# A decoder layer on one core: where the turned probabilities of the cross attention land in PSUM, one comparison behind a key copy, and the latent values in later steps

## The chip, the core and the metric

The kernel runs on one core of one Trainium2 chip. The metric is the device time of one execution in microseconds; the median of three runs is given. The float32 work is the same before and after the change.

## The reference, cut to what matters

For each of 8 batch rows of 256 tokens with 256 channels:

```
a    = x + attention(x)          # 16 heads: latent keys, 64 selected keys, window keys, gated sum
x1   = layernorm(a)
x2   = layernorm(x1 + cross(x1, ctx))   # 16 heads of width 16, 256 x 256 probabilities each
out  = layernorm(x2 + experts(x2))      # 8 experts, 1024 wide, mixed by a router

cross: q = x1 Wq + bq, k = ctx Wk + bk, v = ctx Wv + bv
       p = softmax(q k' / 4) per head ; out = concat(p v) Wo + bo
latent values of the self attention: v1 = rms(x w_ckv) w_dv     # 256 x 512 per row
```

## The kernel before

One program holds an attention stage over the 8 batch rows and an expert stage after it. The order of the work on every engine is written out by hand, as generators for TensorE (`pe`), VectorE (`dve`), ScalarE (`act`) and GpSimd (`pool`), which meet in semaphores. A row has three parts: `front(i)` (projections, rotary parts, selection of 64 tokens, turned keys and queries), `heads(i)` (16 heads of self attention) and `cross(i)` (16 heads of cross attention, in steps h = 0 to 19). `interleave` runs one step of the front of row i+1 after each step of the last heads and of the cross part of row i, but for three steps (`BREATHERS`). From h = 16 on, the first heads of row i+1 run too. The last row has no front of another row beside it; the first transposes and router scores of the expert stage run there instead.

PSUM has eight banks: S0 to S3, T0, T1, O and X. A `BankPlan` numbers the uses of each bank; a writer waits until the use before it has been read (`free_S0`), a reader until the bank is full (`full_S0`). One cross head h goes through these steps:

- TensorE writes the scores of two heads at once, of h and h+1 for even h, into S0 and S1 (`scores_x`, line 1380 of the profile, `ps_S<-kx_sb,qx_sb`). It waits for both banks.
- VectorE reads them, takes the maximum (lines 1294 and 1300), ScalarE exponentiates (871), VectorE inverts the sum (1174), GpSimd scales (651).
- TensorE turns the probabilities of head h in step h+3 (`turn_probs_x`, 1715), always into the single bank T0 (in the last row into T0 and T1 in turn, by the plan `late`).
- ScalarE copies them to SBUF (883), or VectorE does for heads 1, 5, 9, 13, 14 and 15 (`VECTOR_TURNS`, 1310). After each four heads TensorE multiplies with the values (`ps_O<-pT_sb,vx`).

Of the front, four things matter. `turn_rows` (1435) turns keys and queries, alternately into X and T1. VectorE copies the keys in T1 out (1012), and in the same steps makes two pairs of comparisons for the selection, `beaten_by(0)` and `beaten_by(1)` (1031, 1033). `latent_values(0)` and `(1)` are products of 32 rows into S3 (1380, `ps_S<-w_qd,latT_sb 32*128`), which ScalarE scales into SBUF (703, `v_sb`). Between them stand three products of one column, the places of the selected tokens (`pos`, `ps_S<-sel,upper`). The products of the selected keys and values (`ps_S<-w_ks,lat`) come later, and last the transposes of the selected keys (`turn_rows(4)`, `ps_X<-ident,rot 64*96`).

Of the kernel before, what the change touches and what calls it, by code (L numbers as in the profile page):

```python
# [16 lines left out]
NB, T, C = 8, 256, 256  # L17
NT = T // P
NC = C // P
NH = 16  # L20
# [139 lines left out]
def block_plan(full, free):  # L160

    plan = BankPlan(full, free)
    for h in range(NH):
        for half in range(2):
            if h >= HEAD_START:
                plan.add(("s", h, half), f"S{2 * (h % 2) + half}")
        for half in range(2):
            plan.add(("pT", h, half), f"T{half}")
    for g in range(4):
        plan.add(("o", g), ("X", "O")[g % 2])  # L170
    plan.add("proj", "S0")
    plan.add("ctxT", "O")
    plan.add("kx", "S0")
    plan.add("vx", "S1")
    plan.add("x1T", "T0")
    plan.add("qx", "S0")
    for h in range(NH):
        plan.add(("sx", h), f"S{h % 2}")
        plan.add(("pxT", h), "T0")
    for g in range(2):  # L180
        plan.add(("ox", g), "O")
    plan.add("projx", "O")


    for n, name in enumerate((
# [5 lines left out]
        plan.add(name, f"S{2 + n % 2}", ahead=True)  # L191
    for n, name in enumerate((
            "xT", ("kwT", 0, 0), ("kwT", 0, 1), ("kwT", 0, 2), "latT", ("kwT", 0, 3),
            *(("kwT", 1, g) for g in range(4)), *(("qT", t, g) for t in range(NT) for g in range(4)),
            ("ksT", 0), ("ksT", 1))):
        plan.add(name, ("X", "T1")[n % 2], ahead=True)
    for h in range(HEAD_START):
        for half in range(2):
            plan.add(("s", h, half), f"S{2 * (h % 2) + half}", ahead=True)
    return plan  # L200
# [68 lines left out]
def attention_stage(nc, outer, block, sh, w):  # L269

    ctx = ExitStack()
    with ctx:
# [8 lines left out]
        plan = block_plan({b: sem(f"full_{b}") for b in BANKS}, {b: sem(f"free_{b}") for b in BANKS})  # L281

        def ps(name):
            return pst[plan.bank(name)]

        LATE_BANKS = ("T0", "T1", "S2", "S3", "X")
        late = BankPlan({b: sem(f"late_full_{b}") for b in LATE_BANKS},
                        {b: sem(f"late_free_{b}") for b in LATE_BANKS})
        for h in range(NH):
            late.add(("pxT", h), f"T{h % 2}")  # L290
        for n, name in enumerate((*(("x2T", j, c) for j in range(EARLY) for c in range(NC)),
                                  *(("route", j) for j in range(EARLY)))):
            late.add(name, ("S2", "S3", "X")[n % 3])

        def px(i, h):

            return (late, ("pxT", h), 0) if i == NB - 1 else (plan, ("pxT", h), i)


        w_first = sb("w_first", [P, NC, PA])  # L300
# [43 lines left out]
        gate = sb("gate_sb", [P, 4])  # L344
# [4 lines left out]
        pos = sb("pos_sb", [P, NT])  # L349
# [3 lines left out]
        rot, qT, kT, v1, vw, vs = sh.rot, sh.qT, sh.kT, sh.v1, sh.vw, sh.vs  # L353
# [337 lines left out]
        def _(act):  # L691
# [6 lines left out]
            def evacuate(i, name, dst, src, scale=None):  # L698
                act.wait_ge(plan.full_sem(name), plan.after(name, i))
                if scale is None:  # L700
                    ins = act.copy(dst, src)  # L701
                else:
                    ins = act.activation(dst, src, ACT.Copy, scale=scale)
                ins.then_inc(plan.free_sem(name), 1)
                return ins

            def front(i):
# [26 lines left out]
                def values_out(name, t, dst, scale):  # L734
                    evacuate(i, (name, t), dst[:, t, :], ps((name, t))[:, :], scale)
# [37 lines left out]
                if i:  # L773
# [5 lines left out]
                absorbed(1)  # L779
                query_turn(0, 0)  # L780
                yield
                values_out("v1", 0, v1, gate[:, 0:1])
                query_turn(0, 2)
                yield

                values_out("v1", 1, v1, gate[:, 0:1])
                query_turn(1, 0)
                yield
                query_turn(1, 2)
# [4 lines left out]
                nope(4)  # L794
                evacuate(i, ("ks", "nv"), vs[:, :], ps(("ks", "nv"))[KEEP:2 * KEEP, :], gate[KEEP:2 * KEEP, 1:2])
                yield
                yield

                evacuate(i, ("ksT", 0), kT[:, 0:8, 0:KEEP],
                         ps(("ksT", 0))[0:QK, :].rearrange("p (h t) -> p h t", h=8))  # L800

# [149 lines left out]
        def _(dve):  # L951
# [21 lines left out]
            def front(i):  # L973
# [35 lines left out]
                def key_turn(t, g):  # L1009
                    f = ("kwT", t, g)  # L1010
                    dve.wait_ge(plan.full_sem(f), plan.after(f, i))
                    dve.tensor_copy(kT[:, 4 * g:4 * g + 4, KEEP + P * t:KEEP + P * t + P],
                                    ps(f)[0:QK, :].rearrange("p (h t) -> p h t", h=4)).then_inc(plan.free_sem(f), 1)
# [16 lines left out]
                def beaten_by(t):  # L1030
                    dve.tensor_scalar(cmp1[:, t, :], srow[:, :], scol[:, t:t + 1], None, ALU.is_gt
                                      ).then_inc(c.step(), 1)
                    dve.scalar_tensor_tensor(cmp2[:, t, :], srow[:, :], scol[:, t:t + 1], tie[:, t, :],
                                             ALU.is_equal, ALU.mult).then_inc(c.step(), 1)
# [66 lines left out]
                dve.tensor_copy(latT[0:QL, 0, :], ps("latT")[0:QL, 0:T])  # L1101
                dve.tensor_copy(latT[:, 1, :], ps("latT")[:, T:2 * T]).then_inc(plan.free_sem("latT"), 1)
                own_scores()
                beaten_by(0)
                yield

                key_turn(0, 3)
                beaten_by(1)
                yield

# [264 lines left out]
        def _(pe):  # L1375
# [9 lines left out]
            for h in range(NH):  # L1385
                last = mm(pst["S0"][0:QL, HD * h:HD * h + HD], stage[:, QL * h:QL * h + QL],
                          stage[:, NH * QL + HD * h:NH * QL + HD * h + HD])
# [25 lines left out]
            def front(i):  # L1413
# [44 lines left out]
                def latent_values(t):  # L1458
                    product(i, ("v1", t), P, HW, [latT[QK:P, 1, P * t:P * t + P]], [w_dv[QK:P, :]])
# [9 lines left out]
                for t in range(NT):  # L1469
                    for c in range(NC):  # L1470
                        last = mm(ps("first")[:, T * t:T * t + PA], xT[:, c, P * t:P * t + P], w_first[:, c, :],
                                  c == 0, c == NC - 1)
# [59 lines left out]
                yield  # L1532

                turn_rows(2, (2, 3))
                latent_values(0)
                pe.wait_ge(sel_sb.sem, sel_sb.at(i, 1))
                pe.wait_ge(plan.free_sem("pos"), plan.before("pos", i))
                mm(ps("pos")[:, 0:1], upper[:, :], sel[:, 0:1])
# [1 line left out]
                mm(ps("pos")[:, 1:2], upper[:, :], sel[:, 1:2], False, True).then_inc(plan.full_sem("pos"), 1)  # L1540
                yield

                latent_values(1)
                turn_rows(3, (0, 1))
                yield

# [16 lines left out]

                selected(("ks", "nv"), [w_ks[:, c, 0, :] for c in range(NC)], [w_vs[:, c, :] for c in range(NC)])
                yield
                yield

                turn_rows(4, (0, 1))

            def scores(i, h):  # L1570
# [245 lines left out]
    def end(turns, f, i):  # L1816

        return turns.free_sem(f), turns.after(f, i)

    last = NB - 1  # L1820
    banks = {"S0": end(plan, ("sx", NH - 2), last), "S1": end(plan, ("sx", NH - 1), last),
             "S2": end(late, ("route", 0), 0), "S3": end(late, ("route", 1), 0), "X": end(late, ("route", 2), 0),
             "T0": end(late, ("pxT", NH - 2), 0), "T1": end(late, ("pxT", NH - 1), 0),
             "O": end(plan, "projx", last)}
# [515 lines left out]
```

## Time and profile before

| | us |
|---|---|
| median of 3 runs (lowest, highest) | 1892.19 (1890.14, 1893.77) |
| the profiled execution, its time | 1895.1 |
| its span, first to last instruction | 1893.4 |
| attention stage, until the first expert product | 1148.2 |
| expert stage | 745.2 |

The profile has for each engine the busy time, for each wait its releaser, and for each instruction a start and a duration. "PEclk" is the TensorE clock granted, as a share of 2.4 GHz: 1.00 or 0.50 at any moment. The time of the profiled execution is 1.7 us more than its span and 2.9 us above the median.

### The profile page before, as it was taken

What the parts mean: (1) busy time and instruction counts of PE and PEld (TensorE: products, weight loads), DVE (VectorE), ACT (ScalarE), POOL (GpSimd) and SP (SyncE); (2) the same over time, 40 slices, a digit from 0 to 9 for tenths busy, and PEclk for the clock granted to TensorE, in tenths of its full rate; (3) what the DMA queues carried; (4) which work ended last, traced back from release to release, by engine and by line L of the source; (5) the groups of instructions that cost most, each with busy time, mean ns of one, the idle gap of its engine ahead of it and who ended that gap; (6) DMA issues with size and microseconds to landing.
All of it is one profiled execution on the core that took longest, in us unless ns stands there. A gap on an engine that the chain in (4) does not pass through costs nothing. (4 is left out here: it accounts for less than half of the span.)

```text
span 1893.4 us, 33996 instructions
## 1 busy us (share of the span) xinstructions
PE 1776.1 (94%) x11560; PEld 1372.9 (73%) x11560; DVE 1167.2 (62%) x3980; ACT 888.8 (47%) x2839; POOL 1040.3 (55%) x1447
## 2 busy tenths in 40 slices
PE   7899999999999998999999979999999999999998
PEld 4565665665765765755756747889999999898997
DVE  4568768868867867867777766444543354436335
ACT  1475765856845846936936863222222222213221
POOL 2354554654744745735735638456565566547643
PEclk9799899999998999999999988899999999999999
DMA  5000000000000000000000001010101011010001
GB/s 167 6 1 7 7 2 7 7 8 7 2 7 7 2 7 7 2 7 7 2 7 1 13 35 45 1 45 1 45 1 45 1 45 45 1 42 4 1 1 45
DMA packets 24492, 32.86 MB, mean 17 GB/s; under 512 B 5048, under 2 KB 20928, under 8 KB 24320
## 3 DMA queue, kind: packets, MB, share of 16 engines
q1 hardware_dynamic: 24320, 30.69, 4.9%
q8 instruction: 93, 1.52, 0.3%
q14 instruction: 79, 0.65, 0.1%
HBM read 28.58 MB, written 2.10 MB: 16 GB/s over the span
## 5 line engine op out<-in xcount | busy, mean ns | idle before, releaser
L1942 POOL TENSOR_TENSOR h_lo<-h_sb,h_hi 128x512 fp32r<-128x512 f32 x256 | 360.3, 1433 | 157.5 <-DVE h_hi L2112 157.5
L1990 ACT ACTIVATE h_sb<-ps_H,b_sb 128x512 f32<-128x512 f32 x256 | 176.1, 688 | 523.2 <-PE ps_H L2149 510.1
L616 POOL TENSOR_TENSOR pr<-pr,rden 128x128 f32<-128x128 f32 (+2 forms) x768 | 307.8, 435 | 117.5 <-DVE rden L1174 117.5
L818 ACT ACTIVATE pr<-sm,nmx 128x128 f32<-128x128 f32 (+2 forms) x768 | 311.6, 411 | 33.0 <-DVE nmx L1193 32.9
L2112 DVE CAST h_hi<-h_sb 128x512 fp32r<-128x512 f32 x256 | 221.4, 879 | 157.5 <-ACT h_sb L1990 156.8
L2149 PE MATMUL ps_Y<-w_hi,h_lo 128*128 128x256 f32 x1024 | 288.0, 281 | 0.0
L2149 PE MATMUL ps_Y<-w_hi,h_hi 128*128 128x256 f32 x1024 | 288.0, 281 | 0.0
L2149 PE MATMUL ps_Y<-w_lo,h_hi 128*128 128x256 f32 x1024 | 287.7, 281 | 0.0
L651 POOL TENSOR_TENSOR pr<-pr,rden 128x256 f32<-128x256 f32 x256 | 156.7, 634 | 218.1 <-DVE rden L1174 218.1
L1185 DVE CUSTOM_DVE_ANT_0 sm<-ps_S,cmask 128x128 f32<-128x128 f32 (+2 forms) x768 | 191.4, 307 | 35.8 <-PE ps_S L1380 26.5
L2094 DVE SCALAR_TENSOR_TENSOR x<-ps_Y,route_t,x 128x256 f32<-128x256 f32 x128 | 61.3, 482 | 235.6 <-PE ps_Y L2149 235.6
L2149 PE MATMUL ps_H<-x_hi,w_hi 128*128 128x512 f32 x512 | 203.4, 397 | 0.1
L2149 PE MATMUL ps_H<-x_lo,w_hi 128*128 128x512 f32 x512 | 202.6, 396 | 0.0
L2149 PE MATMUL ps_H<-x_hi,w_lo 128*128 128x512 f32 x512 | 202.5, 396 | 0.0
L2149 PEld LDWEIGHTS ps_Y<-w_hi,h_hi 128*128 128x128 f32 x1024 | 194.5, 190 | 1.3
L2149 PEld LDWEIGHTS ps_Y<-w_lo,h_hi 128*128 128x128 f32 x1024 | 194.5, 190 | 1.2
L2149 PEld LDWEIGHTS ps_Y<-w_hi,h_lo 128*128 128x128 f32 x1024 | 194.5, 190 | 0.0
L871 ACT ACTIVATE pr<-sm,nmx 128x256 f32<-128x256 f32 x256 | 128.1, 502 | 88.9 <-DVE nmx L1300 88.9
L1603 PE MATMUL ps_T<-ident,pr 128*128 128x128 f32 (+1 forms) x1024 | 135.3, 275 | 21.1 <-DVE pT_sb L1205 6.7
L1603 PEld LDWEIGHTS ps_T<-ident,pr 128*128 128x128 f32 (+1 forms) x1024 | 109.8, 133 | 52.7 <-issue 36.6
L818 ACT ACTIVATION_READ_ACCUMULATOR pr<-sm,nmx 128x1 f32 x768 | 147.0, 191 | 0.0
L1380 PE MATMUL ps_S<-latT_sb,qT_sb 128*128 128x128 f32 (+1 forms) x512 | 129.6, 336 | 5.2 <-ACT kT_sb L701 4.2
(246 smaller groups left out, 3281.3 us busy)
## 6 DMA issues: line engine op xcount, KB each, us to landing
w_raw<-in_W SPq DMA_DIRECT2D x16, 1024.0 KB, 6.2
xin<-in_x SPq DMA_DIRECT2D x8, 256.0 KB, 2.9
cin<-in_ctx SPq DMA_DIRECT2D x8, 256.0 KB, 2.6
out<-x SPq DMA_DIRECT2D x4, 512.0 KB, 3.0
w_kw<-in_wink SPq DMA_DIRECT2D x2, 768.0 KB, 6.6
w_ks<-in_selk SPq DMA_DIRECT2D x2, 768.0 KB, 10.0
w_qd<-in_dq SPq DMA_DIRECT2D x1, 576.0 KB, 4.8
w_vw<-in_winv SPq DMA_DIRECT2D x1, 512.0 KB, 8.0
```

The costliest lines, as they stand in the source:

```text
L616: last = pool.tensor_tensor(p_, p_, rden[:, h % 2, n:n + 1].to_broadcast([P, width]), ALU.mult)
L651: last = pool.tensor_tensor(p_, p_, rden[:, h % 2, q:q + 1].to_broadcast([P, T]), ALU.mult)
L818: last = act.activation(pr[:, h % PR_SLOTS, a:a + width], sm[:, h % 2, a:a + width], ACT.Exp, bias=nmx[:, h % 2, n:n + 1], scale=ATT_SCALE ...
L871: last = act.activation(prx[:, h % PR_SLOTS, T * q:T * q + T], smx[:, h % 2, T * q:T * q + T], ACT.Exp, bias=nmx[:, h % 2, q:q + 1], scale ...
L1185: ins = dve.tensor_tensor_reduce(out=sm[:, h % 2, a:a + width], in0=ps(f)[:, off:off + width], in1=cmask[:, m:m + width], scale=1.0, scala ...
L1380: return pe.matmul(out, lhsT, rhs, start=start, stop=stop)
L1603: last = pe.transpose(ps(f)[0:width, dst:dst + P], p[:, a:a + width], ident[:, :])
L1942: pool.tensor_tensor(h_lo[:, s % 2, ht, :], h_sb[:, ht % 4, :], h_hi[:, s % 2, ht, :].bitcast(F32), ALU.subtract).then_inc(lo_sb.sem, 1)
L1990: ins = act.activation(h_sb[:, ht % 4, :], pst[plan.bank(f)][:, :], ACT.Relu, bias=b1[:, 2 * i + s // NCH, ht:ht + 1])
L2094: dve.scalar_tensor_tensor(x2[:, tile, :], pst[plan.bank(f)][:, 0:C], rt[:, 2 * i + s // NCH, tile:tile + 1], x2[:, tile, :], ALU.mult, AL ...
L2112: dve.tensor_copy(h_hi[:, s % 2, ht, :], h_sb[:, ht % 4, :]).then_inc(hi_sb.sem, 1)
L2149: return pe.matmul(out_, lhsT, rhs, start=start, stop=stop)
```

## The change

Three edits. (1) In the bank plan the turned probabilities of the even cross heads 0 to 12 go to S0 in place of T0, between the score pairs that use S0; the odd heads and head 14 stay on T0. In the last row the heads that stay now alternate over T0 and T1, and the even ones go to S0 as well. (2) VectorE's `beaten_by(0)` moves from the step of the latent copy to the next step, behind the key copy `key_turn(0, 3)`. (3) The two latent values and their copies move from the steps around `pos` to the two steps after the selected keys and values, and in the plan of S2 and S3 they stand last.

```diff
@@ block_plan
-    for h in range(NH):
-        plan.add(("sx", h), f"S{h % 2}")
-        plan.add(("pxT", h), "T0")
+    for k in range(NH + 3):
+        if k < NH and k % 2 == 0:
+            plan.add(("sx", k), "S0")
+            plan.add(("sx", k + 1), "S1")
+        if k >= 3:
+            h = k - 3
+            plan.add(("pxT", h), "S0" if h % 2 == 0 and k < NH else "T0")
...
-            ("v1", 0), "pos", ("v1", 1), "xsel", ("ks", "ab"), ("ks", "nv"))):
+            "pos", "xsel", ("ks", "ab"), ("ks", "nv"), ("v1", 0), ("v1", 1))):
@@ attention_stage
-        for h in range(NH):
-            late.add(("pxT", h), f"T{h % 2}")
+        ONE_BANK = [h for h in range(NH) if plan.bank(("pxT", h)) == "T0"]
+        for n, h in enumerate(ONE_BANK):
+            late.add(("pxT", h), f"T{n % 2}")
...
-            return (late, ("pxT", h), 0) if i == NB - 1 else (plan, ("pxT", h), i)
+            return (late, ("pxT", h), 0) if i == NB - 1 and h in ONE_BANK else (plan, ("pxT", h), i)
@@ ScalarE, front
-                values_out("v1", 0, v1, gate[:, 0:1])
                 query_turn(0, 2)
                 yield
-                values_out("v1", 1, v1, gate[:, 0:1])
                 query_turn(1, 0)
...
                 evacuate(i, ("ks", "nv"), vs[:, :], ps(("ks", "nv"))[KEEP:2 * KEEP, :], gate[KEEP:2 * KEEP, 1:2])
                 yield
-                yield
+                values_out("v1", 0, v1, gate[:, 0:1])
+                yield
+                values_out("v1", 1, v1, gate[:, 0:1])
@@ VectorE, front
                 own_scores()
-                beaten_by(0)
                 yield
                 key_turn(0, 3)
+                beaten_by(0)
                 beaten_by(1)
@@ TensorE, front
                 turn_rows(2, (2, 3))
-                latent_values(0)
                 pe.wait_ge(sel_sb.sem, sel_sb.at(i, 1))
...
-                latent_values(1)
                 turn_rows(3, (0, 1))
...
                 selected(("ks", "nv"), ...)
                 yield
-                yield
+                latent_values(0)
+                yield
+                latent_values(1)
                 turn_rows(4, (0, 1))
```

How the instructions stand now. First TensorE in cross steps 8 and 9, from the query transposes into T1 to those into X: `w_qd` is a latent value, `sel` the places, `ident,pr` turned probabilities of head 6. Before:

```order
L1435 MATMUL ps_T1<-ident,rot_57 128x128 [waits free_T1]
L1435 MATMUL ps_T1<-ident,rot_57 128x128 x3
L1380 MATMUL ps_S3<-w_qd_49,latT_sb 128x512 [waits free_S3]
L1380 MATMUL ps_S2<-sel,upper 128x1 [waits free_S2,sel_sb]
L1380 MATMUL ps_S2<-sel,ones 128x1
L1380 MATMUL ps_S2<-sel,upper 128x1
L1715 MATMUL ps_T0<-ident,pr 128x128 [waits free_T0,prob_sb]
L1715 MATMUL ps_T0<-ident,pr 128x128 x3
L1380 MATMUL ps_S3<-w_qd_49,latT_sb 128x512 [waits free_S3]
L1435 MATMUL ps_X<-ident,rot_57 128x128 [waits rope_out,free_X,free_S2,free_S3]
```

The same place in the changed kernel:

```order
L1441 MATMUL ps_T1<-ident,rot_57 128x128 [waits free_T1]
L1441 MATMUL ps_T1<-ident,rot_57 128x128 x3
L1386 MATMUL ps_S3<-sel,upper 128x1 [waits free_S3,sel_sb]
L1386 MATMUL ps_S3<-sel,ones 128x1
L1386 MATMUL ps_S3<-sel,upper 128x1
L1722 MATMUL ps_S0<-ident,pr 128x128 [waits free_S0,prob_sb]
L1722 MATMUL ps_S0<-ident,pr 128x128 x3
L1441 MATMUL ps_X<-ident,rot_57 128x128 [waits rope_out,free_X,free_S2,free_S3]
```

Both latent values are gone from here, and head 6 goes to S0. Second, TensorE from cross step 14 (heads 11 and 12 turned) to the transposes of the selected keys. Before:

```order
L1715 MATMUL ps_T0<-ident,pr 128x128 [waits free_T0,prob_sb]
L1715 MATMUL ps_T0<-ident,pr 128x128 x3
L1715 MATMUL ps_T0<-ident,pr 128x128 [waits free_T0,prob_sb]
L1715 MATMUL ps_T0<-ident,pr 128x128 x3
L1380 MATMUL ps_O<-pT_sb,vx 32x256 [waits free_T0,free_O]
L1380 MATMUL ps_O<-pT_sb,vx 32x256 x7
L1435 MATMUL ps_X<-ident,rot_57 96x64 [waits free_X,sel_nope,rope_out]
```

The same place in the changed kernel:

```order
L1722 MATMUL ps_T0<-ident,pr 128x128 [waits free_T0,prob_sb]
L1722 MATMUL ps_T0<-ident,pr 128x128 x3
L1386 MATMUL ps_S3<-w_qd_49,latT_sb 128x512 [waits free_S3]
L1722 MATMUL ps_S0<-ident,pr 128x128 [waits free_S0,prob_sb]
L1722 MATMUL ps_S0<-ident,pr 128x128 x3
L1386 MATMUL ps_O<-pT_sb,vx 32x256 [waits free_T0,free_S0,free_O]
L1386 MATMUL ps_O<-pT_sb,vx 32x256 x7
L1386 MATMUL ps_S2<-w_qd_49,latT_sb 128x512 [waits free_S2]
L1441 MATMUL ps_X<-ident,rot_57 96x64 [waits free_X,sel_nope,rope_out]
```

The first latent value now stands between the turned heads 11 and 12, the second behind the value products of heads 8 to 11. Third, VectorE around the scores of cross heads 2 and 3, in the changed kernel alone:

```order
L1033 TENSOR_REDUCE scol<-cmp1 128x2 [waits dve_front_chain]
L1300 ISA sm,mx<-ps_S0,sm 128x256 [waits full_S0,dve_front_chain,exp_done]
...
L1306 TENSOR_SCALAR nmx<-mx 128x2 [waits free_S1]
L1018 COPY kT_sb_59<-ps_T1 96x4x128 [waits full_T1]
L1037 TENSOR_SCALAR cmp1<-srow,scol 128x256
L1039 SCALAR_TENSOR_TENSOR cmp2<-srow,scol,tie 128x256
L1037 TENSOR_SCALAR cmp1<-srow,scol 128x256
L1039 SCALAR_TENSOR_TENSOR cmp2<-srow,scol,tie 128x256
```

Before, one pair of comparisons stood between the first two of these rows, ahead of the scores and the key copy; now both pairs stand behind the copy.

## Rows read from the trace of the kernel before

**Rows 1.** The page: busy time, share and instructions of each engine.

```profile
PE 1776.1 (94%) x11560; PEld 1372.9 (73%) x11560; DVE 1167.2 (62%) x3980; ACT 888.8 (47%) x2839; POOL 1040.3 (55%) x1447
```

**Rows 2.** Waits of TensorE, whole span: total us, times, longest us.

```profile
PE ps_T L1715 <- DVE pT_sb L1310: 14.3, 21, 0.8
...
PE ps_T L1435 <- DVE kT_sb L1012: 9.3, 8, 1.2
...
PE ps_T L1715 <- ACT pT_sb L883: 5.8, 7, 0.8
```

**Rows 3.** Batch rows as windows: start, end, length, TensorE busy, granted clock, DMA.

```profile
157.00:295.40 138.40, 128.25 (x851) 0.96 0.02 5
295.40:429.10 133.70, 123.59 (x854) 1.00 0.02 6
...
563.10:701.80 138.70, 128.31 (x851) 0.96 0.02 5
...
835.40:972.30 136.90, 126.82 (x853) 0.98 0.02 6
...
1100.10:1148.20 48.10, 38.69 (x231) 0.76 0.00 1
```

**Rows 4.** Windows at three of the four falls of the clock, columns as above.

```profile
189.40:199.70 10.30, 10.30 (x49) 0.50 0.11 28
...
868.70:875.50 6.80, 6.80 (x33) 0.50 0.02 6
...
1005.20:1012.00 6.80, 6.80 (x33) 0.50 0.00 1
```

**Rows 5.** Timeline, TensorE, second batch row: start, us, what, idle before, releaser.

```profile
304.89 0.61 PE L1435 MATMUL ps_T<-ident,rot 128*96 128x128 f32 x4 [1.24 <-DVE kT_sb L1012]
...
312.31 0.63 PE L1715 MATMUL ps_T<-ident,pr 128*128 128x128 f32 x4 [0.84 <-DVE pT_sb L1310]
...
315.08 1.98 PE L1380 MATMUL ps_S<-w_qd,latT_sb 96*128 96x512 f32 x4 [0.48 <-ACT rot L717]
```

**Rows 6.** Timeline, TensorE, later in the same batch row.

```profile
324.19 1.12 PE L1380 MATMUL ps_S<-w_qd,latT_sb 32*128 32x512 f32 x2
325.24 0.38 PE L1380 MATMUL ps_S<-sel,upper 128*128 128x1 f32 x2
...
326.46 0.63 PE L1715 MATMUL ps_T<-ident,pr 128*128 128x128 f32 x4 [0.39 <-DVE pT_sb L1310]
...
338.29 0.63 PE L1715 MATMUL ps_T<-ident,pr 128*128 128x128 f32 x4 [0.80 <-DVE pT_sb L1310]
...
343.26 0.63 PE L1715 MATMUL ps_T<-ident,pr 128*128 128x128 f32 x4 [0.82 <-ACT pT_sb L883]
...
347.20 0.46 PE L1380 MATMUL ps_S<-latT_sb,qT_sb 128*128 128x128 f32 x2 [0.60 <-ACT kT_sb L701]
```

**Rows 7.** Timeline, VectorE and ScalarE, same batch row.

```profile
301.15 0.35 DVE L1031 TENSOR_SCALAR cmp<-srow,scol 128x256 f32<-128x256 f32 x1
...
301.82 0.41 DVE L1294 CUSTOM_DVE_ANT_0 sm<-ps_S,sm 128x256 f32<-128x256 f32 x1
...
319.88 0.67 DVE L995 TENSOR_TENSOR rt<-ps_S,cs 128x512 f32<-128x512 f32 x1
...
325.40 0.67 ACT L703 ACTIVATE v_sb<-ps_S,gate_sb 128x512 f32<-128x512 f32 x1
...
346.38 0.56 ACT L701 COPY kT_sb<-ps_X 96x512 f32<-96x512 f32 x1
```

**Rows 8.** Timeline, last batch row.

```profile
1112.94 0.56 ACT L883 COPY pT_sb<-ps_T 128x512 f32<-128x512 f32 x1
1112.96 1.13 PE L1380 MATMUL ps_S<-kx_sb,qx_sb 32*128 32x256 f32 x8 [1.82 <-DVE mx L1294]
...
1131.06 1.13 PE L1380 MATMUL ps_S<-kx_sb,qx_sb 32*128 32x256 f32 x8 [1.18 <-DVE mx L1294]
...
1134.31 1.04 ACT L945 CAST w_hi<-w_raw 128x1024 fp32r<-128x1024 f32 x1
```

More of the change, by code:

```diff
@@ L1820, in attention_stage @@
     last = NB - 1
-    banks = {"S0": end(plan, ("sx", NH - 2), last), "S1": end(plan, ("sx", NH - 1), last),
+    banks = {"S0": end(plan, ("pxT", NH - 4), last), "S1": end(plan, ("sx", NH - 1), last),
              "S2": end(late, ("route", 0), 0), "S3": end(late, ("route", 1), 0), "X": end(late, ("route", 2), 0),
```

## The prediction

> **What bounds the kernel now.** I read the page first. TensorE is busy for 94% of the span [rows 1], so a gain must come from its waits or from its clock. The expert stage (745.2 us) is untouched. In the attention stage the list of waits shows where TensorE stands still [rows 2]: 14.3 + 5.8 us before it turns cross probabilities, because the one bank T0 still holds the head before, and 9.3 us before it turns a key block, because VectorE has not copied the last one out of T1. The counts (21, 7 and 8 or 7 per kind) say that the same waits come back in each of the seven batch rows with a following front. The windows by batch row say the same in another way [rows 3]: a row takes 133.7 us at clock 1.00, and 138.4, 138.7 and 136.9 us where the clock was at half for a part. These parts are whole stretches at 0.50, that is 1.2 GHz: 10.3 us, or 6.8 us twice [rows 4]; a fourth, in the row from 563.1, is of the length of the first. So there are two things to win: waits of a few tenths, and falls of the clock that cost 4.7, 5.0 and 3.2 us each, and 3.2 more for the last one, which is as long as the third: 16.1 us in all.
>
> **The change, part by part.** I follow one batch row, the second, by the timeline of TensorE.
>
> *The comparison.* VectorE now starts the scores of heads 2 and 3, and behind them the key copy, at 301.15 and not at 301.82 [rows 7]: 0.67 us earlier. The wait of 1.24 us before the key transposes [rows 5] shrinks to 0.57. The comparisons themselves come back behind the copy, before VectorE's next work, so VectorE has no less to do. Gain here 0.67.
>
> *What holds it at 0.6 for a while.* From there VectorE has hardly a gap until its last rotary product of this stretch, at 319.88 for 0.67 us [rows 7], and TensorE's next query product needs the bank that this one frees. VectorE starts this chain some 0.6 us earlier, so that point comes 0.6 earlier, whatever waits TensorE lost before. Two of them do go (0.84 and 0.48 [rows 5]). The first only moves: head 2 may now be turned at once, but the score pair behind it needs S0, which ScalarE has yet to copy (about 0.7 us for the end of the transposes and the copy). The second goes because that copy is earlier. Neither counts in the sum.
>
> *The latent values leave the steps around the places.* Each costs 1.05 us from its start to the next (324.19 to 325.24 [rows 6]); two are 2.1. The wait of 0.39 for T0 behind them goes too. But they covered something: the query transposes that follow need X, copied by ScalarE, and T1, copied by VectorE, whose own clock hands are only 0.6 early. I count 0.9 us of new waits at these two, from when those copies end. At the score pair of heads 10 and 11 TensorE is early by 0.6 + 2.1 + 0.4 - 0.9 = 2.2 us.
>
> *Late steps.* The wait of 0.80 before head 10 goes: its bank S0 was read long before. The one of 0.82 before head 12 (1.0 from start to start) is filled by the first latent value, 1.05. The second adds 1.05: 2.2 + 0.8 + 1.0 - 2.1 = 1.9 us early. The last wait, 0.60 before the next row's first scores [rows 6], has ScalarE's key copy in it (346.38, 0.56). ScalarE now does two latent copies of 0.67 [rows 7] in these steps, the second directly ahead of that copy; I find its end 1.9 to 2.0 early, so the wait stays near 0.6. The last steps' S3 and S2 are free in time: the rotary products of the selected keys end about 0.8 us before the first latent value wants S3. Behind this point every engine is early by the same amount, and the rest of the row keeps its waits. **Per row 1.95 us, in seven rows 13.7.** Bounds of the row: 0.6, if VectorE's chain holds throughout, and 3.3, the sum of the four waits for T0 and the part of T1's that I take (0.84 + 0.39 + 0.80 + 0.82, and 0.67), less small ones.
>
> *The last row.* Nothing of a front runs beside it, and 48.1 us are mostly latency. There T0 and T1 in turn never held the heads back; now every even head shares S0 with the scores. The pair of heads 6 and 7 starts at 1112.96, when VectorE has read the banks; in the changed kernel it also waits for ScalarE's copy of head 2, which ran 1112.94 to 1113.50 [rows 8]: 0.6 late. The next pairs wait likewise, and ScalarE's weight casts of 1.04 us stand ahead of two of those copies [rows 8], so the pair at 1131.06 may be 4 us late. ScalarE's exponentials had slack behind it, and I carry about half through to the end: **3 us lost**, between 0.5 (the first pair alone) and 5.
>
> *The clock.* In all four rows that show a fall, and in these alone the row is long, it comes at 32 to 33 us behind the first cross scores: right behind latent value, one-column places, wait, turned head, latent value [rows 6]. The three other rows ran the same without a fall. The change takes both latent values and one wait out of that stretch, which then holds transposes with three short waits. It also makes a new thin stretch: the second latent value, the short transposes of the selected keys, one turned head and the wait of 0.6. It is shorter than the old one, so I expect a fall in one or two of seven rows and not in four. **I take 9 of the 16.1 us back**; bounds 16 and minus 12 (falls of 4 us in all seven rows: 28 against 16.1).
>
> The Trainium skill ("TensorE: Matmul & The Clock Gate", "A second HAM failure mode: psum-queue depth-cycling") says that short idles between groups, from cycling through PSUM banks, make the clock swing between its two levels. By that rule fewer waits for a bank leave fewer falls, but the new waits at X and T1 in the same stretch could keep them all; the sum would then be 1881.5. The trace agrees in part: the falls come behind a stretch with such a wait, yet longer waits elsewhere in the row brought none.
>
> The start-up front of the first row has no cross part beside it; the moved products lie there under GpSimd's rotary sums. I count nothing.
>
> Sum: -13.7 - 9 + 3 = -19.7 us. Against the profiled execution, 1895.1 us, that is 1875.4. The median of before is 2.9 lower, as other executions have other falls of the clock, and the change is judged by the median: **1872.5 us**.
>
> **The rivals.**
> - *Waits go, the clock stays as it was* (four falls, by new waits in the old stretch or by the new thin one). For it: the stretch keeps the places and gets two waits. 1892.2 - 13.7 + 3 = 1881.5. Chance 0.17.
> - *VectorE holds all back.* Only the comparison counts: 7 x 0.6 = 4.2, less 3 in the last row, and no fall saved: 1891. For it: VectorE's chain sets four of the meeting points. Against it: after 320.6 us VectorE waits for TensorE's scores again. Chance 0.06.
> - *Slower: S0 makes the score pairs late.* Each pair from head 4 on must wait until ScalarE has copied the even head before. It bites where the copy ends after TensorE reaches the pair; for heads 6 and 7 it does (a pause of 0.7 in place of 0.84), for heads 8, 10 and 14 there is over 1 us of other work between, for 12 and 13 only 0.2 us of margin. If ScalarE runs later than I find by more than 1 us, six pairs in seven rows wait some 0.5: 21 us. With the last row's 3 and the 13.7 gained: about 1902. Chance 0.05.
> - *Slower or equal by the clock alone*: a fall in every row: -13.7 + 12 + 3, 1893.5. Chance 0.06.
> - *No place for the gain*: a later wait takes up most of it. Each engine is shifted alike at the row's end, so little speaks for it: 1889. Chance 0.02.
>
> **How the numbers follow.** My case has the other 0.64, with a range of its own of 1864 to 1881: waits between 10 and 17, clock between 4 and 16, last row 0.5 to 5. With the first rival inside, 1863 to 1884 leaves two in ten out, above all on the slow side. A measurement of this kernel tells 0.2% (3.8 us) from no change. Faster by more: my case and the first rival and a little of the others, 0.82; same 0.11 (the clock rival, VectorE and the last one among them); slower 0.07.
>
> **What the profile of the changed kernel would show.** The wait of the key transposes on VectorE near 0.6; waits of `ps_T` for its copies gone from heads 6, 10 and 12; a wait of some 0.7 before the scores of heads 6 and 7; batch rows of about 131.8 us at clock 1.00; windows at 0.50 in fewer rows, and then near 46 to 50 us behind the first cross scores; a last row of about 51 us. I would be wrong if rows at clock 1.00 took over 133, or if the score pairs showed waits on ScalarE's copies in each step.

## The result and the profile after

Measured beside each other, the kernel before took 1892.01 us (median; 1890.14 to 1893.77) and the changed one 1863.19 us (1860.3 to 1866.08): a ratio of 0.9848, with an interval of 0.983 to 0.9866. That is 9.3 us below my number and only 0.2 us inside the range of 1863 to 1884; the 1864 that I had as the least of my own case is missed. The profiled execution of the changed kernel took 1863.8 us, span 1862.1; so 31.3 us of span are to be explained, not 28.8.

The page's busy times of the changed kernel, the line that answers to [rows 1]:

```profile
PE 1756.3 (94%) x11560; PEld 1359.8 (73%) x11560; DVE 1168.3 (63%) x3980; ACT 888.6 (48%) x2839; POOL 1042.2 (56%) x1447
```

TensorE runs as many instructions as before and is busy 19.8 us less. No product was taken away, so these 19.8 us are the clock's: the same work at 2.4 GHz and not at 1.2. The rest of the 31.3, some 11.5, are waits. VectorE, ScalarE and GpSimd are busy as before.

The list of TensorE's waits in the changed kernel (total us, times, longest us), which answers to [rows 2]:

```profile
PE ps_S L1386 <- issue: 7.3, 10, 1.1
...
PE ps_X L1441 <- ACT qT_sb L706: 6.9, 8, 1.3
...
PE ps_T L1441 <- DVE kT_sb L1018: 5.8, 8, 0.8
...
PE ps_S L1386 <- DVE kT_sb L1169: 3.5, 8, 0.9
PE ps_S L1722 <- DVE mx L1300: 3.4, 9, 0.5
PE ps_S L1386 <- DVE pr L1001: 2.9, 8, 0.4
PE ps_S L1386 <- ACT pT_sb L889: 2.8, 2, 2.1
...
PE ps_T L1722 <- DVE pT_sb L1316: 0.4, 1, 0.4
```

The 14.3 us in 21 waits for VectorE's copy of T0 are one wait of 0.4, and the 5.8 us for ScalarE's are gone. The key transposes wait 5.8 and not 9.3. In their place stand new, smaller ones: for X (6.9; 1.3 before), before score pairs (7.3 with the releaser "issue", which means that the profile shows none; 0.72 of it in each row with a front is the pair of heads 6 and 7, below), and for S0 until its scores are read (3.4). The wait before the next row's scores isn't new: it was 4.2 for ScalarE's copy and 0.9 for VectorE's, and is 3.5 for VectorE's.

The same batch rows as windows, with the columns of [rows 3], and under them two falls of the clock, as in [rows 4]:

```profile
281.20:412.90 131.70, 123.19 (x851) 1.00 0.02 6
676.70:809.70 133.00, 124.67 (x851) 0.99 0.02 5
809.70:942.70 133.00, 124.68 (x851) 0.99 0.02 6
1065.40:1117.00 51.60, 40.19 (x230) 0.77 0.00 1
726.70:730.10 3.40, 3.40 (x12) 0.50 0.00 0
859.80:863.20 3.40, 3.40 (x12) 0.51 0.00 0
```

A row at full clock takes 131.7 us, 2.0 less than the 133.7 of [rows 3]; with the marks to the hundredth, the second row went from 133.62 to 131.72, 1.90 less. Two of seven rows have a fall, 50 us behind their first cross scores and 3.4 us long, where four had one at 32 us, 6.8 or 10.2 long. Unlike in [rows 3], the last row is longer: 51.6 for 48.1.

By marks in the trace the 31.3 us divide so:

| stretch (marks: first cross scores of a row, first expert product) | before | after | difference |
|---|---|---|---|
| start to the first row's cross scores | 157.0 | 149.5 | -7.5 |
| seven rows with a following front | 943.1 | 915.9 | -27.2 |
| last row | 48.1 | 51.6 | +3.5 |
| expert stage | 745.2 | 745.1 | -0.1 |

The 27.2 divide again by a second profile of the changed kernel, told below, in which no row fell: there the seven rows take 913.5. Before, they take 943.1 less 16.1 of falls, 927.0. So the waits gave 13.5 and the clock 13.7.

TensorE's timeline in the second batch row, which answers to [rows 5, 6] (this batch row starts at 281.2 and not at 295.4):

```profile
290.15 0.61 PE L1441 MATMUL ps_T<-ident,rot 128*96 128x128 f32 x4 [0.77 <-DVE kT_sb L1018]
...
297.89 1.13 PE L1386 MATMUL ps_S<-kx_sb,qx_sb 32*128 32x256 f32 x8 [0.72 <-issue]
...
309.37 0.28 PE L1386 MATMUL ps_S<-sel,upper 128*128 128x1 f32 x2
...
309.73 0.36 PE L1386 MATMUL ps_S<-sel,upper 128*128 128x1 f32 x2
309.95 0.63 PE L1722 MATMUL ps_S<-ident,pr 128*128 128x128 f32 x4
311.39 0.63 PE L1441 MATMUL ps_X<-ident,rot 128*128 128x128 f32 x4 [0.81 <-ACT qT_sb L706]
312.25 0.65 PE L1441 MATMUL ps_T<-ident,rot 128*128 128x128 f32 x4 [0.23 <-DVE qT_sb L1024]
...
331.02 0.46 PE L1386 MATMUL ps_S<-latT_sb,qT_sb 128*128 128x128 f32 x2 [0.39 <-DVE kT_sb L1169]
```

The turned head behind the places now goes to S0 (`ps_S<-ident,pr`) and waits for nothing. Of the waits that the prediction named, that of the key transposes is 0.77 (it said 0.57), that before the scores of heads 6 and 7 0.72 (0.7), and those at X and T1 together 1.04 (0.9). For the 0.72 the profile names no releaser; ScalarE's copy out of S0 ran from 297.20 to 297.79, and the pair starts at 297.89. The wait before the next row's scores is 0.39, and it comes from VectorE's half of the selected keys, no longer from ScalarE's.

### The profile page after: what moved, and what is told of

It reads as the page before. It is cut to its first block and busy times, and to the rows that moved or that the text cites. A ratio compares the mean times of both kernels' runs of the same rounds, so it can differ in the third digit from the quotient of the medians.

```text
span 1862.1 us, 34004 instructions
## 1 busy us (share of the span) xinstructions
PE 1756.3 (94%) x11560; PEld 1359.8 (73%) x11560; DVE 1168.3 (63%) x3980; ACT 888.6 (48%) x2839; POOL 1042.2 (56%) x1447
## 5 line engine op out<-in xcount | busy, mean ns | idle before, releaser
L1191 DVE CUSTOM_DVE_ANT_0 sm<-ps_S,cmask 128x128 f32<-128x128 f32 (+2 forms) x768 | 191.6, 308 | 35.1 <-PE ps_S L1386 19.7
L1386 PE MATMUL ps_S<-kT_sb,qT_sb 96*128 96x320 f32 (+1 forms) x512 | 134.6, 386 | 0.0
```

The source lines that it names most:

```text
L1191: ins = dve.tensor_tensor_reduce(out=sm[:, h % 2, a:a + width], in0=ps(f)[:, off:off + width], in1=cmask[:, m:m + width], scale=1.0, scala ...
L1386: return pe.matmul(out, lhsT, rhs, start=start, stop=stop)
```

## The experiments

### Each edit alone, and the last row apart

**The comparison alone.** The kernel before, with one edit:

```diff
                 own_scores()
-                beaten_by(0)
                 yield
                 key_turn(0, 3)
+                beaten_by(0)
                 beaten_by(1)
```

> The kernel before with the comparison behind the key copy and nothing else. Theory of the sum (waits are separate terms): the wait of the key transposes on VectorE falls from 1.24 to 0.6-0.8 us in seven rows, 7 x 0.6 = 4 us, falls of the clock as before and the start-up as before (first cross scores at 157.0 us): 1887 to 1888. Rival (the gain of this edit is taken up at the next wait for T0, since VectorE's chain is what moves): the first wait shrinks, the one before head 2 grows, 1891 to 1892.

1876.92 us (12 runs), ratio 0.9937 (0.9912 to 0.9963): far more than the 4 us I had put on it. The windows of its first two rows:

```profile
153.60:291.60 138.00, 128.32 (x851) 0.96 0.02 5
291.60:424.80 133.20, 123.57 (x853) 1.00 0.02 6
```

A row at full clock gained 0.5 us, where I expected 0.6. The rest is the clock: one row of seven fell in this profile, not four, and the start-up and the last row, 3.4 and 2.8 us shorter than before, had less time at half clock too.

**The banks alone**: the edits of the bank plan and the last row's table, nothing else.

> The kernel before with the bank edit alone (even heads to S0, last row on T0 and T1). Theory: the waits before heads 6, 10 and 12 go, but the late steps are then held by GpSimd's rotary sums for the selected keys, so a row gains about 0.9 us and not 2.2, 6 us in all; the last row loses 3.5; latent values stay, so the clock falls as often as before: about 1889. Rival (the waits for T0 are what lets the clock fall): no or few windows at 0.50 in rows 1 to 7, 15 us less, about 1875.

1879.26 us (10 runs), ratio 0.9939 (0.9919 to 0.996). Rows at full clock of 132.8, 0.9 less, and a last row of 51.2 us, both as the theory has them; three rows with a fall. The time is 10 us under the theory's 1889: fewer rows fell in this profile than in the one before, and its start-up is 3.1 us shorter. TensorE's timeline ahead of the first fall, then a window over its last 4.1 us, and the fall:

```profile
316.46 0.38 PE L1385 MATMUL ps_S<-sel,upper 128*128 128x1 f32 x2
...
316.93 0.36 PE L1385 MATMUL ps_S<-sel,upper 128*128 128x1 f32 x2
317.15 0.64 PE L1720 MATMUL ps_S<-ident,pr 128*128 128x128 f32 x4
317.72 1.52 PE L1385 MATMUL ps_S<-w_qd,latT_sb 32*128 32x512 f32 x2
```

```profile
314.20:318.30 4.10, 4.10 (x26) 1.00 0.00 0
318.40:328.60 10.20, 10.20 (x46) 0.50 0.09 27
```

Head 6 goes to S0 and waits for nothing, the profile shows no pause of TensorE in the 4.1 us ahead, and the clock falls all the same. So the wait of 0.39 for T0 isn't needed for a fall.

**The latent values alone**: the two products, their two copies, and their two names in the plan.

> The kernel before with only the latent values moved. Theory (the products of 32 rows around the one-column places are what the clock falls behind, in the start-up too): the first cross scores come at about 149.7 us, no falls at 32 us of a row, waits of the rows unchanged in sum (the wait before head 6 grows by 1.05, the one before head 12 is filled): about 1872, rows of 133.7 at clock 1.00. Rival (start-up gain and clock were chance, or need the bank edit too): start-up at 157.0 and falls as before, 1890 to 1892.

1880.49 us (11 runs), ratio 0.9949 (0.9934 to 0.9965), and I was wrong in the main point: three rows still fell at 32 us behind the first cross scores. TensorE's timeline ahead of the first of them, and the window of the fall:

```profile
712.38 0.28 PE L1381 MATMUL ps_S<-sel,upper 128*128 128x1 f32 x2
...
712.75 0.36 PE L1381 MATMUL ps_S<-sel,upper 128*128 128x1 f32 x2
714.76 0.63 PE L1717 MATMUL ps_T<-ident,pr 128*128 128x128 f32 x4 [1.65 <-DVE pT_sb L1311]
```

```profile
715.90:722.70 6.80, 6.80 (x33) 0.50 0.06 8
```

With the latent values away but the head still on T0, the time that they took is a wait of 1.65 us for T0. That is also why this edit alone gives a row only 0.3 us (its second row takes 133.34, before 133.62; the 133.6 and 0.1 that the next expectations name come from its fourth row). The start-up is another matter: the first cross scores start at 149.7.

**The last row apart**: the changed kernel, but in the last row every head is turned on T0 and T1 in turn, as before, and S0 holds scores alone.

```diff
-        ONE_BANK = [h for h in range(NH) if plan.bank(("pxT", h)) == "T0"]
-        for n, h in enumerate(ONE_BANK):
-            late.add(("pxT", h), f"T{n % 2}")
+        for h in range(NH):
+            late.add(("pxT", h), f"T{h % 2}")
...
-            return (late, ("pxT", h), 0) if i == NB - 1 and h in ONE_BANK else (plan, ("pxT", h), i)
+            return (late, ("pxT", h), 0) if i == NB - 1 else (plan, ("pxT", h), i)
```

The counts of S0's uses in the last row, which the semaphores wait for, are lowered to match (left out above).

> The changed kernel, but in the last row all turned heads alternate over T0 and T1 as before, and S0 holds scores alone there. Theory (the last row lost 3.5 us to S0): its 51.6 us go back to about 48, 1859.5 in all. Rival (those 3.5 us are another fall of the clock, 17.1 us at 0.50 in this row, by chance): the row stays at 50 to 52, 1863.

1855.15 us (5 runs, 1852.85 to 1859.7), ratio 0.9815 (0.9786 to 0.9844), the lowest median of all; its interval still touches that of the changed kernel (0.983), and the last row's window says more. The window of its last row, and then TensorE's waits for ScalarE's copy in the last row of the changed kernel, which this kernel does not have:

```profile
1064.70:1111.20 46.50, 35.21 (x230) 0.85 0.00 1
```

```profile
1079.01 2.08 PE L1386 MATMUL ps_S<-kx_sb,qx_sb 32*128 32x256 f32 x8 [0.72 <-ACT pT_sb L889]
...
1102.07 2.00 PE L1386 MATMUL ps_S<-kx_sb,qx_sb 32*128 32x256 f32 x8 [2.07 <-ACT pT_sb L889]
```

The rival, chance in the clock, has a part: this row has a clock of 0.85 in the mean, that of the changed kernel 0.77 (23.9 us at half), and the row before the change 0.76 with 48.1 us. At the same clock the shared S0 costs 3.5 us (51.6 against 48.1), and against this row 5.1.

### Do the gains of a row add up?

> The kernel before with the comparison and the banks changed, the latent values in their old steps. The question is whether the gains of a row add up: rows at clock 1.00 took 133.7 us before, 133.2 with the comparison alone, 132.8 with the banks alone, 133.6 with the latent values alone and 131.7 with all three, so the three edits give 0.5 + 0.9 + 0.1 = 1.5 apart and 2.0 together. Theory 1 (the edits help each other through the latent values: they fill the waits that the banks leave in the late steps): rows of 132.3 us here, the plain sum of two. Theory 2 (the comparison and the banks help each other, the latent values give nothing to a row): rows of 131.8 us. On the clock: if the latent values' old steps are what makes it fall, windows at 0.50 stay at some 31 us behind the first cross scores in two to four rows; if it is the timing of the whole row, any number from none to seven. Time 1872 to 1879 us.

> The kernel before with the banks and the latent values changed, the comparison still ahead of the key copy. Theory 1 (banks and latent values work together): rows at clock 1.00 of 132.2 us or less, that is 131.7 + 0.5, and the comparison adds its 0.5 as it does alone. Theory 2 (the comparison is what lets the others count): rows of 132.7, the sum of banks and latent values. VectorE's chain of the middle of the row bounds the gain there, so if it held the row, this kernel could not be under 133.1. Windows at 0.50 at about 50 us behind the first cross scores in two rows if the new thin stretch makes them. Last row about 51 us. Time 1868 to 1874 us.

> The kernel before with the comparison and the latent values changed, every turned head on T0 as before. Theory 1 (the waits for T0 hold the row unless the banks change): rows at clock 1.00 of 133.1 us, the sum of 0.5 and 0.1. Theory 2 (comparison and latent values help each other): rows of 132.6 or less. By the clock term of my prediction the old stretch without the latent values is free of falls; with the latent values alone it had three at 32 us behind the first cross scores, so I expect zero to three here. First cross scores of the first row at about 149.5 us if the latent values' place sets the start-up. Last row about 47 us. Time 1872 to 1880 us.

None of the three times was met: 1882.0, 1864.7 and 1868.9 us were measured. The rows at full clock came as forecast or nearly so; falls, start-up and last row make the rest. One row at full clock of each, in the same order:

```profile
289.10:421.40 132.30, 123.37 (x853) 1.00 0.02 6
```

```profile
280.00:412.20 132.20, 123.23 (x853) 1.00 0.02 6
```

```profile
284.90:417.80 132.90, 123.11 (x853) 1.00 0.02 6
```

Twelve of the fourteen profiles (the first column in the words of the edits; the other two stand in the next part):

| kernel | median us, ratio (interval) | first cross scores | row at full clock | rows of 7 with a fall | last row |
|---|---|---|---|---|---|
| before | 1892.0 | 157.0 | 133.6 | 4, at +32 to +33 | 48.1 |
| before, again | 1893.9 (one run) | 154.1 | 133.6 | 5, at +32 to +33 | 48.0 |
| comparison | 1876.9, 0.9937 | 153.6 | 133.2 | 1, at +32 | 45.3 |
| banks | 1879.3, 0.9939 | 153.9 | 132.8 | 3, at +32, +33 and +51 | 51.2 |
| latent | 1880.5, 0.9949 | 149.7 | 133.3 | 3, at +32, one of them again at +107 | 49.5 |
| comparison, banks | 1882.0, 0.9945 (0.9914 to 0.9976) | 156.8 | 132.3 | 2, at +31, one of them again at +55 | 51.0 |
| banks, latent | 1864.7, 0.984 (0.9809 to 0.9871) | 147.8 | 132.2 | 1, at +50 | 51.4 |
| comparison, latent | 1868.9, 0.9861 (0.9834 to 0.9888) | 147.2 | 132.9 | 2, at +30 to +31 | 47.9 |
| all three | 1863.2, 0.9848 (0.983 to 0.9866) | 149.5 | 131.7 | 2, at +50 | 51.6 |
| all three, again | 1861.0 (one run) | 147.7 | 131.7 | 0 | 51.2 |
| all three, last row apart | 1855.2, 0.9815 (0.9786 to 0.9844) | 147.3 | 131.7 | 3, at +50 | 46.5 |
| the same, own scores too | 1860.6, 0.9833 (0.9806 to 0.9859) | 149.3 | 131.7 | 0 | 45.4 |

(+32 is 32 us behind the row's first cross scores. Row at full clock: the second, or the fifth where the second fell.) The comparison gives 0.5 whatever stands beside it (133.6 to 133.2; 132.8 to 132.3; 132.2 to 131.7; 133.3 to 132.9). The banks give 0.9 alone and 1.2 with the latent values moved, the latent values 0.3 alone and 0.6 with the banks: theory 1, with 0.3 of help and not the 0.5 that it started from. Nothing is left for theory 2, as the comparison with the latent values is the plain sum of the two. Where the 0.3 lies can be read in the late steps: with the banks alone TensorE waits 0.8 before head 12, for GpSimd's probabilities, and 0.9 before the transposes of the selected keys; the latent values fill both. Three other readings of the table:

- Start-up: with the latent values in place it is 153.6 to 157.0 in five profiles, with them moved 147.2 to 149.7 in seven.
- Last row: with even heads on S0 51.0 to 51.6 in five profiles, without it 45.3 to 49.5 in seven.
- Falls: the number at +32 is not one edit's. In this table it becomes 0 only where banks and latent values are both changed (five profiles, 35 rows). The falls at +50 aren't the moved latent values' alone: the banks alone had one at +51.

**Before and after once more**, unchanged, for their profiles:

> The kernel before once more, unchanged, with a profile: how much do the places of the clock's falls and the start-up move from one execution to the next? If the falls belong to the program, the rows from 157.0, 563.1 and 835.4 us and the last but one are the long ones again and the first cross scores start at 157 us; if chance decides, other rows are long and the start-up differs by several us. Time 1890 to 1896 us.

> The kernel after once more, unchanged, with a profile: the same question as for the kernel before, how much the clock's falls move from one execution to the next. Rows at clock 1.00 should again take 131.7 us, the first cross scores start at 147 to 150 us, the last row take 51 to 52 us, and falls of 3.4 us come at 50 us behind the first cross scores in zero to four rows. 1860 to 1866 us.

Before: a fifth row fell, the one from 426.2, and the first 157.0 us are 154.1 with another place of the falls. So part of a difference of one row or one start-up is chance from one execution to the next; the falls come back in the rows they had before and in one more.

### What makes the clock fall at +32

Both kernels are the one before with the same four products more in each front, whose result is not used. One has them ahead of the places:

```diff
                 pe.wait_ge(plan.free_sem("pos"), plan.before("pos", i))
+                for c in range(NC):
+                    mm(ps("pos")[:, T:2 * T], w_first[:, c, 0:P], xT[:, c, :])
                 mm(ps("pos")[:, 0:1], upper[:, :], sel[:, 0:1])
```

> The kernel before, and in each front four more products of 128x256 ahead of the one-column places (their result is not used): about 1.0 us of TensorE's work, which stands in the stretch behind which the clock falls. In the two profiles of the kernel before there, four and five of seven rows fell at 32 to 33 us behind the first cross scores. Theory 1 (the thin stretch makes the falls): none of seven rows falls there; rows of 134.7 us; 8 x 1.0 more work and some 16 us of falls less than before: about 1884 us. Theory 2 (chance, or the length of the row, decides which rows fall, not what stands at the places): three or more rows still fall there, and the time is 1896 to 1900 us.

and the control has them some 15 us earlier in the row, ahead of `queries(0, 0)`:

> The control of the run before: the same four products, but at the first query products of a front, 14 us behind the first cross scores, where TensorE has whole products on both sides. They can fill most of the wait of 0.84 behind them, so the row becomes 133.9 to 134.7 us. Theory 1 (the thin stretch makes the falls): three to five of seven rows fall at 32 to 34 us as before; time 1893 to 1899 us. Theory 2 (the length of the row decides): as few falls as in the run with the products at the places.

At the places: 1875.34 us, ratio 0.9919 (0.9891 to 0.9948). At the queries: 1893.9 us, ratio 1.0015 (0.9993 to 1.0037). TensorE's timeline at the places in the first, a row at full clock, and then the row of the control with a fall, and that fall:

```profile
314.90 1.12 PE L1380 MATMUL ps_S<-w_qd,latT_sb 32*128 32x512 f32 x2
315.95 1.13 PE L1380 MATMUL ps_S<-xT_sb,w_first 128*128 128x256 f32 x4
316.92 0.28 PE L1380 MATMUL ps_S<-sel,upper 128*128 128x1 f32 x2
317.06 0.36 PE L1380 MATMUL ps_S<-sel,ones 128*128 128x1 f32 x2
317.28 0.36 PE L1380 MATMUL ps_S<-sel,upper 128*128 128x1 f32 x2
317.51 0.64 PE L1717 MATMUL ps_T<-ident,pr 128*128 128x128 f32 x4
```

```profile
559.00:697.80 138.80, 129.16 (x855) 0.96 0.02 5
```

```profile
591.50:601.70 10.20, 10.20 (x49) 0.50 0.10 28
```

With 1 us of whole products in this stretch none of seven rows fell, and the wait of 0.39 for T0 is filled too; they took 134.0 us at full clock, only 0.4 more. With the same products elsewhere four fell, at +33. So more work made the kernel 16.7 us faster, at one of the two places tried: what stands in this stretch matters, as theory 1 has it, and the length of the row alone (theory 2) doesn't explain it. The time is 9 us under theory 1's 1884: the row is 0.7 shorter than expected, and the start-up is 152.1 us and not 157.0, as the clock didn't fall there either until 65.6. Two things stay open. The comparison alone leaves the stretch as it was and had one fall, so the stretch alone doesn't decide. And the runs don't say which part of it matters: the wait isn't needed (the banks alone), nor are the latent values (moved alone).

### VectorE's other part ahead of the key copy

To "the last row apart", one more edit:

```diff
-                own_scores()
                 yield
                 key_turn(0, 3)
+                own_scores()
                 beaten_by(0)
```

> The kernel after with the last row's turned heads on T0 and T1, and also VectorE's own_scores (1.05 us) put behind the key copy, ahead of the two comparisons. The wait of 0.77 before the key transposes that is left should go. Theory 1 (the wait of the key transposes is worth its length, as the first comparison alone gave 0.5 of its 0.67 us per row): rows of 131.0 to 131.3 us and 1850 to 1852 us. Theory 2 (VectorE's chain to its last rotary product holds the row from here, since VectorE has no less to do): the wait goes, rows stay at 131.7, time 1855 us.

1860.62 us (5 runs, 1855.21 to 1862.47), ratio 0.9833 (0.9806 to 0.9859); rows of 131.7 to 131.8. TensorE's timeline in the second row:

```profile
289.29 0.61 PE L1449 MATMUL ps_T<-ident,rot 128*96 128x128 f32 x4
...
297.07 1.13 PE L1394 MATMUL ps_S<-kx_sb,qx_sb 32*128 32x256 f32 x8 [0.77 <-ACT pT_sb L897]
...
301.58 0.63 PE L1730 MATMUL ps_S<-ident,pr 128*128 128x128 f32 x4 [1.07 <-DVE mx L1308]
```

The wait of the key transposes is gone and the row gains nothing: the turned head at 301.58 now waits 1.07 for VectorE (0.35 in the changed kernel). Theory 2, for the row. VectorE has no less to do, and what TensorE gains at one wait it gives back at the next. The time isn't theory 2's 1855: this profile is the fastest of five runs (1855.21), the others took 1859 to 1862 at a lower granted clock (0.986 to 0.988 against 0.992), and no profile shows where.

## Why the prediction was right, and where it was not

**The waits, -13.7 (measured -13.5).** The size held: 1.95 us a row forecast, 1.90 measured. So did the steps, each a little too large. TensorE's score pairs in the second row, counted from its first cross scores, before and after:

| score pair | before | after | earlier | forecast |
|---|---|---|---|---|
| heads 8 and 9 | 26.23 | 25.75 | 0.48 | 0.6 |
| heads 10 and 11 | 33.66 | 31.65 | 2.01 | 2.2 |
| heads 14 and 15 | 45.27 | 42.43 | 2.84 | 3.0 |
| next row's first | 133.62 | 131.72 | 1.90 | 1.95 |

The comparison gave 0.5 and not 0.67, and the run with `own_scores` shows that VectorE's chain allows no more. That a latent value fills the wait before head 12 is in the prediction's steps, and the pairs show the help: banks and latent values give 1.4 together, 0.9 and 0.3 apart.

**The clock, -9 (measured -13.7).** Both places were right: the old stretch no longer falls, in 14 rows of two profiles, and falls come at +50. The term was undersized because falls there are 3.4 us long and cost 1.3 us each, where my bound had 4 us, and they came in two rows of seven or none. The step behind it was half right. I had put the falls down to the latent values and the wait in the stretch. Taking out the wait alone (the banks alone) leaves three falls, two of them at +32 to +33, and taking out the latent values alone, which leaves a wait of 1.65 us in their place, three; only both edits, or 1 us of products more, ended them. The Trainium skill ("TensorE: Matmul & The Clock Gate", "A second HAM failure mode: psum-queue depth-cycling") puts such swings down to short idles between groups; the runs here agree with it at most in part. The banks alone fell behind 4.1 us without a pause; the changed kernel waits 0.81 and 0.23 at X and T1 in the same stretch, more than before in sum, and doesn't fall there; and the wait at the key transposes, 0.77 or 1.24, brings no fall in any kernel. So idle time in the stretch doesn't explain the falls, and what does stays open. So does their number: the comparison alone, which changes nothing in the stretch, had one and not four. Its 12 runs were 15 us under before in the median, ten of them between 1874 and 1880 and two at 1892 and 1897, so it is not one odd profile; whether the row's changed timing spares the other rows was not tried. So the direction of this term was well founded, and its size was in part luck.

**Start-up, 0 (measured -7.5).** This term I had put at nothing, and it is most of my error. I had looked only at where the products go: under GpSimd's rotary sums, and there they do lie. But they left a place ahead of the selection's places and of `ktmp`'s product, on which the selected keys and so the first scores wait, and they ran at half clock there. TensorE before, then after, then the selected keys of the kernel with products added at the places:

```profile
54.40 2.07 PE L1380 MATMUL ps_S<-w_qd,latT_sb 32*128 32x512 f32 x2
56.39 0.58 PE L1380 MATMUL ps_S<-sel,upper 128*128 128x1 f32 x2
...
57.76 2.07 PE L1380 MATMUL ps_S<-w_qd,latT_sb 32*128 32x512 f32 x2
...
64.96 3.13 PE L1380 MATMUL ps_S<-w_ks,lat 128*64 128x512 f32 x9
```

```profile
54.19 0.28 PE L1386 MATMUL ps_S<-sel,upper 128*128 128x1 f32 x2
...
57.75 2.36 PE L1386 MATMUL ps_S<-w_ks,lat 128*64 128x512 f32 x9
```

```profile
59.80 2.36 PE L1380 MATMUL ps_S<-w_ks,lat 128*64 128x512 f32 x9
```

The selected keys start 7.2 us earlier. About 2.1 of it are the latent values themselves (1.05 each at full clock); the rest is mostly the clock, at half for 13.7 us from 52.9. The third kernel shows it: there the latent values stand in their old place with 1 us of products more, the clock stays up, and the selected keys start 5.2 us earlier than before. The clock fell between 52.8 and 56.8 us in all six profiles with the latent values in place and no products added at the places, and in none of the seven with them moved; those seven start their cross scores at 148.4 in the mean, the five of the table with them in place at 155.1. So some 6.7 of the 7.5 go with the edit. Why the fall began at 52.8 or 52.9 in two profiles, ahead of the first latent value, and lasted 13.7 and not 6.8 us, is not shown; these two have the longest start-ups, 157.0 and 156.8.

**The last row, +3 (measured +3.5).** Right in size and in place: the pair of heads 6 and 7 waits 0.72 (forecast: 0.6 late), and a wait of 2.07 stands before the pair of heads 14 and 15. That pair is 5.6 us late and not 4, counted from the row's first cross scores, and 3.5 of it come through to the end. Undone, the row is 46.5 us, with less of it at half clock.

**The sum.** -7.5 - 13.5 - 13.7 + 3.5 - 0.1 = -31.3 against my -19.7: 7.5 of the 11.6 are the start-up and 4.7 the clock, less what the last row and the waits differ. None of the rivals came true. In a row with a front S0 made one score pair late by 0.72, the one I had counted; the two waits that the list puts down to ScalarE's copy, 2.8 us, lie in the last row.

## What to carry to other kernels

Read the stretch ahead of a fall of the clock as you read a wait: filling it with work can be worth more than the work costs (here 16.7 us for 1 us a row), and taking out one part of it, the latent values or the wait, left falls here. When a product is moved in a loop's body, follow it once through the first pass, where nothing runs beside it and it may stand on the chain that starts everything. And test edits in pairs: two of these were worth 1.1 a row apart and 1.4 together, and a bank plan that helps seven rows cost the eighth 3.5 us until it was exempted. Compare like rows, too: the third row of a kernel takes 0.3 to 0.4 us more than the second in every profile without a fall there.

## What the runs showed of the hardware that I had not expected

- 1.0 us more of TensorE's products in each front made the kernel 16.7 us faster (1875.34 against 1892.05): in the profile the clock stays at 2.4 GHz in all seven rows, which take 13.3 us less, and the start-up takes 4.9 less.
- The clock can fall behind a stretch in which the profile shows TensorE without a pause (the banks alone: busy for 4.10 of the 4.10 us before 318.3), and can stay up behind one with more waiting than before (1.04 us in the changed kernel).
- The same program falls in four rows in one execution and in five in the next, and its start-up moves by 2.9 us; single profiles of falls have to be compared with that in mind.
- A fall costs by its length: 10.2 us at 1.2 GHz cost a row 4.7 to 5.1, 6.8 us 3.2 to 3.3, 3.4 us 1.3 to 1.7.
